# One-hot written in fp32 behind the merge, ScalarE's widening cast dropped, and the row-by-row fetch of one tile extended to every super of a graph attention kernel

## The reference

```python
h = jnp.maximum(_layernorm(x, axis=-1), 0.0)
# in _L0_gnn_ref(h, edge_index, edge_attr_64, W_node, W_edge, a):
h = (node_features @ W_node.T).reshape(num_nodes, H, HD)
e = (edge_features @ W_edge.T).reshape(num_edges, H, HD)
h_src, h_tgt = h[src], h[tgt]
att = jnp.sum(jnp.concatenate([h_src, h_tgt, e], axis=-1) * a, axis=-1)
att = jnp.where(att > 0, att, 0.2 * att)
m = jnp.maximum(jax.ops.segment_max(att, tgt, num_segments=num_nodes), 0.0)
ex = jnp.exp(att - m[tgt])
denom = jax.ops.segment_sum(ex, tgt, num_segments=num_nodes) + (num_edges - deg)[:, None] * jnp.exp(-m)
w = ex / denom[tgt]
h_prime = jax.ops.segment_sum(w[:, :, None] * h_src, tgt, num_segments=num_nodes)
return x + h_prime.reshape(num_nodes, H * HD)
```

## Time and profile before

| | before |
|---|---|
| median of 3 runs | 2087.7 us (2086.22 to 2089.43) |
| the profiled execution | 2090.56 us, its span 2088.7 us |
| GpSimd busy | 1542.5 us (74%) |
| VectorE busy | 1575.2 us (75%) |
| TensorE busy | 1460.6 us (70%), mean granted clock 0.628 |
| ScalarE busy | 768.6 us (37%) |
| bytes moved | 230.42 MB, 110 GB/s in the mean |

### The profile page before, as it was taken

How to read it: one execution, slowest core, us unless ns; L and a number is a source line. 1 busy time by engine, 2 the same in 40 slices (tenths; PEclk the granted TensorE clock), 3 DMA queues, 4 the chain that set the end, 5 groups by cost and what they waited for, 6 DMA issues and landing times.

```text
span 2088.7 us, 46636 instructions
## 1 busy us (share of the span) xinstructions
PE 1460.6 (70%) x8371; PEld 1227.2 (59%) x8372; DVE 1575.2 (75%) x4485; ACT 768.6 (37%) x2304; POOL 1542.5 (74%) x1635
## 2 busy tenths in 40 slices
PE   6456867686867776676676676677677677677685
PEld 6445656565656555565565565566566565566564
DVE  8778888787886776776776786786776786786777
ACT  7733433333343243243243243243243243243333
POOL 7777777777777777777777777777777777777770
PEclk9756767666665666566655665555655555665656
DMA  9953344343343334334334334334334333334331
GB/s 277 311 151 109 97 114 116 95 117 93 97 117 104 101 96 111 91 96 112 91 96 112 92 95 112 92 96 111 92 96 110 93 96 111 92 96 110 92 94 29
DMA packets 131275, 230.42 MB, mean 110 GB/s; under 512 B 45539, under 2 KB 90231, under 8 KB 124215
## 3 DMA queue, kind: packets, MB, share of 16 engines
q0 software_dynamic: 51968, 109.76, 23.5%
q1 hardware_dynamic: 44075, 87.75, 12.9%
q10 hardware_dynamic: 34932, 30.38, 4.5%
HBM read 182.03 MB, written 45.71 MB: 109 GB/s over the span
## 4 chain that ended last, share of the span: by engine, by line
POOL 54%; issue 22%; DVE 8%; PE 8%; ACTq 2%; ACT 2%; DMA 1%; DVEq 1%; POOLq 1%; SPq 0%
POOL gath L578 54%; PE bank_rn L1416 3%; PE bank_p L1473 2%; PE bank_w L1473 2%; DVE bank_rn L868 1%; DVE vals L988 1%; ACTq L339 1%; DVE zz L619 1%; ACT gath L1149 1%; PE bank_rn L1424 1%; DMA resets<-ef 1%; ACTq L94 1%; DVEq L94 0%; DVE vals L627 0%; SPq L455 0%
## 5 line engine op out<-in xcount | busy, mean ns | idle before, releaser
L578 POOL DMA_INDIRECT gath<-h_table,idx x1576 | 1495.2, 949 | 484.5 <-issue 478.7
L1473 PEld LDWEIGHTS bank_p<-vals,onehot 128*128 128x128 f32 x1664 | 382.9, 331 | 89.9 <-DVE vals L988 50.7
L1473 PE MATMUL bank_p<-vals,onehot 128*128 128x137 f32 x1664 | 414.0, 442 | 2.6 <-DVE vals L988 2.3
L1263 ACT ACTIVATE ab<-ab_log 128x8 f32<-128x8 f32 x209 | 43.5, 208 | 943.8 <-DVE ab_log L915 832.7
L1473 PEld LDWEIGHTS bank_w<-vals,onehot 128*128 128x128 f32 x1664 | 326.4, 287 | 94.4 <-DVE vals L988 73.0
L1473 PE MATMUL bank_w<-vals,onehot 128*128 128x137 f32 x1664 | 354.2, 393 | 23.8 <-DVE vals L988 23.3
L1449 PE MATMUL bank_s<-s_live,onehot_bits 128*128 128x24 bf16 x1672 | 79.1, 181 | 358.6 <-ACT onehot_bits L1291 358.5
L1416 PEld LDWEIGHTS bank_rn<-w_edge_bd,ef 128*128 128x128 f32 x1664 | 300.0, 282 | 15.1 <-DMA ef<-in_edges 15.1
L1416 PE MATMUL bank_rn<-w_edge_bd,ef 128*128 128x8 f32 x1664 | 294.9, 319 | 14.8 <-DMA ef<-in_edges 14.8
L1449 PEld LDWEIGHTS bank_s<-s_live,onehot_bits 128*128 128x128 bf16 x1672 | 74.2, 109 | 384.8 <-ACT onehot_bits L1291 380.4
L880 DVE SCALAR_TENSOR_TENSOR onehot_bits<-bank_w,tables,zz 128x1024 bf16 (+1 forms) x209 | 268.3, 1284 | 24.1 <-issue 5.1
(11 more groups left out here) (189 smaller groups left out, 1637.3 us busy)
## 6 DMA issues: line engine op xcount, KB each, us to landing
ef<-in_edges SPq DMA_DIRECT2D x52, 1024.0 KB
gath<-h_table SPq DMA_DIRECT2D x3256, 0.5 KB
out_x<-x_all ACTq DMA_DIRECT2D x210, 128.0 KB
gath<-h_table,idx POOLq DMA_INDIRECT x1576
gath<-h_table ACTq DMA_DIRECT2D x1480, 0.5 KB
x_all<-in_x SPq DMA_DIRECT2D x14, 448.0 KB, 12.3
out_x<-x_all SPq DMA_DIRECT2D x14, 448.0 KB
h_table<-gath SPq DMA_DIRECT2D x11, 462.0 KB
```

Of the source, the lines that this page charges most:

```text
L578: e.indirect_dma_start(gath[:, q * GPS + g, t * ROW:(t + 1) * ROW], None, table, bass.IndirectOffsetOnAxis(idx[:, q, g * TILES + t:g * TIL ...
L1473: ins = e.matmul(half_p[q], onehot[q][:, t, :], vals[q][:, t, :], start=(t == 0), stop=(t == TILES - 1))
```

## The change

- VectorE writes the one-hot straight into the fp32 buffer that TensorE reads. The bf16 copy, `widened` on ScalarE and its semaphore s_of are gone.
- The one-hot moves from before `normalise` to behind `merge`, ahead of `rescale`. `past_window` moves from behind `merge` to right behind `normalise`, ahead of vals.
- HAND_QS takes in q = 0: supers 4, 8, ..., 48 are handed too, 49 instead of 37. SyncE issues 80 rows a super (28, 28, 24), ScalarE 48 (12, 12, 12, 12).
- ScalarE's 12 rows of a step come in two portions: offsets of all 12 loaded and 4 rows issued (`rows_ahead`) before `factors`, 8 rows (`rows_behind`) at the end of the step. `store` moves from the step's end to right behind `matched`, ahead of these rows.
- Before the first one-hot VectorE waits for ScalarE's last use of that memory in the first phase.

```diff
--- before.py
+++ after.py
@@ -68,11 +68,11 @@
 LAST_TILES = -(-(N_EDGES - (GROUPS - 1) * GROUP) // P)
 LAST_LANDED = (GPS - 1) * TILES + LAST_TILES
 HAND_FIRST = 3
-HAND_QS = (1, 2, 3)
+HAND_QS = (0, 1, 2, 3)
 HANDED = [b for b in range(HAND_FIRST, SUPERS) if b % RING in HAND_QS]
 HAND_SLOT = GPS - 1
-SP_PARTS, ACT_PARTS = (32, 28, 28), (8, 8, 8, 16)
-EDGES_AT = 1
+SP_PARTS, ACT_PARTS = (28, 28, 24), (12, 12, 12, 12)
+EDGES_AT, ACT_AHEAD = 1, 4
 SP_ROWS, ACT_ROWS = sum(SP_PARTS), sum(ACT_PARTS)
 assert SP_ROWS + ACT_ROWS == P and HAND_FIRST % RING == RING - 1 and RING - 1 in HAND_QS
 ROW_BYTES = 4 * ROW
...
@@ -331,10 +330,13 @@
 
             e.sem_inc(passed, 1)
 
-        def rows_by_hand(e, landed, q, first, count):
-
-            offs = load(nc, e, hand_offs[0:1, q, first:first + count],
+        def row_offsets(e, q, first, count):
+
+            return load(nc, e, hand_offs[0:1, q, first:first + count],
                         [WINDOWS * P * ROW_BYTES - ROW_BYTES] * count)
+
+        def rows_by_hand(e, landed, q, first, offs):
+
             for k, off in enumerate(offs):
                 e.dma_start(gath[first + k:first + k + 1, q * GPS + HAND_SLOT, 0:ROW].bitcast(U8),
                             table_bytes[:, bass.ds(off, ROW_BYTES)]).then_inc(landed[q], 16)
...
@@ -510,7 +512,8 @@
                     if k == EDGES_AT and to_come:
                         next_edges(b)
                     if by_hand:
-                        rows_by_hand(e, d_hand_sp, next_q, sum(SP_PARTS[:k]), rows)
+                        first = sum(SP_PARTS[:k])
+                        rows_by_hand(e, d_hand_sp, next_q, first, row_offsets(e, next_q, first, rows))
 
             next_edges(0)
             wait(e, n_hand, 1)
...
@@ -878,7 +881,7 @@
             def one_hot(buf, slot, offset, col):
 
                 e.scalar_tensor_tensor(
-                    out=onehot_b[buf][:, :, :],
+                    out=onehot[buf][:, :, :],
                     in0=ring_p[:, bass.ds(offset, P)].rearrange("p (a j) -> p a j", a=1)
                     .to_broadcast([P, TILES, P]),
                     scalar=base[:, bass.ds(col, 1)],
...
@@ -970,9 +973,6 @@
                         in1=zs[:, ZEND:ZDST].rearrange("p (t o) -> p t o", o=1).to_broadcast(
                             [P, TILES, HEADS]), op0=ALU.max, op1=ALU.mult).then_inc(s_mc, 1)
 
-                    wait(e, s_of, s)
-                    s_col = s + 3
-                    one_hot(1 - q, *((slot_b, off_b) if q == 0 else (slot_c, off_c)), s_col)
                     if q == 0:
                         slot_c, off_c, w_past0, w_past1, slot_d, off_d = load(
                             nc, e, dve_rec[0:1, bass.ds(u, 1), :].rearrange(
...
@@ -983,6 +983,7 @@
                         beside[q][0]()
 
                     normalise(s, s_1)
+                    past_window((w_past0, w_past1)[q], s, s_1)
                     wait(e, s_ex, s_1)
                     vh = vals[q][:, :, 0:DEG].rearrange("p t (h c) -> p t h c", c=HV)
                     e.tensor_tensor(
...
@@ -997,8 +998,9 @@
                         beside[q][1]()
 
                     merge(q, s, s_1)
-                    past_window((w_past0, w_past1)[q], s, s_1)
-
+
+                    s_col = s + 3
+                    one_hot(1 - q, *((slot_b, off_b) if q == 0 else (slot_c, off_c)), s_col)
                     rescale(q, s, s_1)
                 e.reg_mov(slot_reg, slot_c)
                 e.reg_mov(slot_ahead, slot_d)
...
@@ -1073,6 +1075,7 @@
             z_columns(0, 0, False)
             wait(e, z_ready, 3)
             off_0, _, slot_1, off_1 = load(nc, e, first_rec[0:1, :], [P, SPARE, SLOTS - 1, P])
+            wait(e, n_terms, TERMS + 2)
             one_hot(0, 0, off_0, 2)
             e.reg_mov(slot_reg, 0)
             e.reg_mov(slot_ahead, slot_1)
...
@@ -1232,15 +1235,14 @@
 
                     live_s2((w_b, w_c)[q], s + 3)
                     matched(s_2)
+                    store((past_0, past_1)[q], s_1)
+                    if beside[q][1]:
+                        beside[q][1]()
+                    factors(s, s_1)
+                    if beside[q][0]:
+                        beside[q][0]()
                     if beside[q][2]:
                         beside[q][2]()
-                    factors(s, s_1)
-                    widened(1 - q, s, s_2)
-                    if beside[q][0]:
-                        beside[q][0]()
-                    if beside[q][1]:
-                        beside[q][1]()
-                    store((past_0, past_1)[q], s_1)
 
             def store(w, s_1):
 
...
@@ -1292,11 +1294,6 @@
                     "p (t c) -> p t c", c=P), ACT.Relu, bias=one[:, :], scale=-1.0
                     ).then_inc(s_e, 1)
 
-            def widened(buf, s, count):
-                wait(e, s_oh, count)
-                wait(e, s_b, s)
-                e.copy(onehot[buf][:, :, :], onehot_b[buf][:, :, :]).then_inc(s_of, 1)
-
             def feed(i, q, last_turn):
                 b, slot0 = i * RING + q, q * GPS
                 final = last_turn and q == RING - 1
...
@@ -1307,20 +1304,35 @@
 
                 next_i, next_q = (i, q + 1) if q + 1 < RING else (i + 1, 0)
 
-                def by_hand(k):
-                    if final or not handed(next_i, next_q):
+                by_hand = not final and handed(next_i, next_q)
+                offs = {}
+
+                def rows_ahead(k):
+
+                    if not by_hand:
                         return
                     if k == 0:
                         wait(e, released, b + 1)
                         settle(e)
                         e.wait_ge(d_hand_offs, (b + 1 - HAND_FIRST) * 16 + 16)
                         settle(e)
-                    rows_by_hand(e, d_hand_act, next_q, SP_ROWS + sum(ACT_PARTS[:k]), ACT_PARTS[k])
+                    first = SP_ROWS + sum(ACT_PARTS[:k])
+                    offs[k] = row_offsets(e, next_q, first, ACT_PARTS[k])
+                    rows_by_hand(e, d_hand_act, next_q, first, offs[k][:ACT_AHEAD])
+
+                def rows_behind(k):
+
+                    if not by_hand:
+                        return
+                    first = SP_ROWS + sum(ACT_PARTS[:k]) + ACT_AHEAD
+                    rows_by_hand(e, d_hand_act, next_q, first, offs[k][ACT_AHEAD:])
+
+                def parts(k, extra=None):
+
+                    return extra, lambda: rows_ahead(k), lambda: rows_behind(k)
 
                 walk(nc, e, bounds, b - 1, pair,
-                     ((None, None, lambda: by_hand(0)),
-                      (lambda: z_places(b, slot0), None, lambda: by_hand(1)),
-                      (None, None, lambda: by_hand(2)), (step_3, None, lambda: by_hand(3))))
+                     (parts(0), parts(1, lambda: z_places(b, slot0)), parts(2), parts(3, step_3)))
 
             wait(e, n_const, N_CONST + 1)
             z_places(0, 0)
```

More of the change, by code:

```diff
@@ L150, in build @@
         bits_mem = sb("onehot_bits", [P, 3, TILES, P], BF16)
-        onehot_b = [bits_mem[:, i, :, :] for i in range(2)]
         onehot_t = bits_mem[:, 2, :, :]
@@ L313, in build @@
             "DVE", "s_", "s2 xy lk dd mc oh v mn da db dg am tp ac dn rc no ou")
-        s_ex, s_de, s_e, s_of, s_ab, s_sl, s_sn, s_un, s_nd = own_sems(
-            "ACT", "s_", "ex de e of ab sl sn un nd")
+        s_ex, s_de, s_e, s_ab, s_sl, s_sn, s_un, s_nd = own_sems(
+            "ACT", "s_", "ex de e ab sl sn un nd")
         s_t, s_a, s_b = own_sems("PE", "s_", "t a b")
@@ L1330, in _ @@
             matched(1)
-            wait(e, s_oh, 1)
-            e.copy(onehot[0][:, :, :], onehot_b[0][:, :, :]).then_inc(s_of, 1)
             z_maxima(0, 0)
```

## The result

The changed kernel takes 2252.5 us, the median of 4 runs (2250.3 to 2254.1); the kernel before took 2088.6 beside it. The ratio is 1.0787, with a 95% interval of 1.0773 to 1.080: slower by 164 us. The forecast was 2263, with a range of 2140 to 2340.

What follows compares the result with a forecast made beforehand. GpSimd's gathers bound the kernel before; a ScalarE-VectorE loop would bound it after. Steps of 8.5, 9.4, 11.8 and 11.2 make 40.9 us a super; 48 supers, turns, start and end give a span of 2264, stated as 2263 (2140 to 2340).

Steps and rivals of the forecast that it cites:

- Which engine sets the pace: Whole kernel: GpSimd bounds it before; after, the consumers do, at 40.9 us a super against GpSimd's 38.75.
- One sign: Profile after: GpSimd's gathers would be held by semaphores of VectorE and TensorE instead of pure issue.
- the first rival: GpSimd stays the bound: 2073 us, needing a consumers' super of at most 36.9 us; chance 0.09 for faster.
- Part 1: GpSimd's chain loses one gather in each of 12 supers: 15 us, a gain where GpSimd stays the bound.
- Part 2: ScalarE loses the 1.03 us cast a step; VectorE's fp32 one-hot takes 1.28 us, its new place costing nothing.
- Parts 3 and 4: ScalarE's 12 rows a step and the earlier store close a loop in series with VectorE: 8.5 us inside a pair.
- a loop turn: Where the loop over supers turns, every fourth super, the boundary adds 2.4 us, 11 times.
- the super without rows: The super after super 50's z_cols, with no rows: 34 us to the next z_cols.
- The page that speaks otherwise: Skill page on issuing engines; by it 12 rows hardly lengthen a step, against 0.335 us per row DMA on ScalarE.
- Half hidden: Loop with bursts of 2.8, offsets 0.7, normalise to store 1.6: 2.6 us a super less, 2138; chance 0.10 for 2090 to 2160.
- Instructions or VectorE add: Loop lengthened by bursts of 3.3 us or a one-hot over 1.9: 2.4 us a super, 2378; chance 0.08 for over 2340.
- Part 5: SyncE's 320 rows per four supers instead of 264 cost nothing, as it waited long and issues over two supers ahead.

Runs made afterwards that it cites:

- e2: Kernel before with the one-hot in fp32 behind merge, no cast and past_window early; rows and store as before: 2099.1 us, ratio 1.0038.
- e5: Changed kernel with past_window back behind merge and the store back at the step's end, rows as changed: 2077.1 us, ratio 0.9949.
- e11: Changed kernel with past_window alone put back behind merge, the store still ahead of the 4 rows: 2596.2 us, ratio 1.2435.
- e8: Changed kernel with all 12 rows of a step ahead of ab, the store still ahead of them: 2465.0 us, ratio 1.1804.
- e10: Changed kernel with 8 rows a step by ScalarE, SyncE still at 80, 16 of 128 rows not fetched: 2078.6 us, ratio 0.996.
- e1: Changed kernel with the store alone put back at the end of ScalarE's step, behind the 8 rows: 2278.2 us, ratio 1.0906.
- e9: Changed kernel with 8 rows a step by ScalarE and 96 a super by SyncE: 2338.0 us, ratio 1.1205.
- e4: Changed kernel with all rows ahead of ab in portions of 10, 10, 10, 18 and the store last: 2185.4 us, ratio 1.0454.
- e12: As e4, changed kernel with rows ahead of ab and store last, but portions of 12, 8, 12, 16: 2078.1 us, ratio 0.9963.

## Why the prediction was right

**Which engine sets the pace** (part one, and the sum): right. z_cols waits for no gathers, ScalarE's line and VectorE make the chain. One sign came only in part: the gathers are hardly held by semaphores, 495.0 of their 594.6 us of idle time are still issue. The limit that the first rival named holds too, to 0.2 us: at paces of 35.6 to 37.6 five kernels came out at 2072 to 2079, at 39.7 the time was 2185.

**Part 1**, 12 gathers less: 1564 for the 1576 of the earlier trace rows. The 15 us were worth nothing in the change and show in the rows alone, 2087.1 - 2072.2 = 14.9.

**Part 2**, one-hot and cast: the 1.28 us were met (1277 ns), and in three of the four steps they lie in the wait for ab. In the scan step live waits for nothing; den, one step on, still waits for others there. "Nothing" for the new place is a small miss, the 8.5 us of e2.

**Parts 3 and 4**, the loop in series. Term by term, from the step shown above, beside the forecast:

| part of a step inside a pair | forecast | measured |
|---|---|---|
| ab to unseen, with 8 rows | 3.0 + 0.1 | 1001.44 - 998.66 = 2.78 |
| unseen to the end of others | 0.3 | 0.31 |
| others to den | 0.15 | 0.14 |
| den to the store | 1.9 | 1.93 |
| the store | 0.4 | 0.39 |
| the store's end to the first row | 1.0 | 1005.55 - 1004.21 = 1.34 |
| 4 rows and the step to ab | 1.65 | 1.60 |
| sum | 8.5 | 8.49 |

That this sum comes out to 0.01 is luck, because two mis-sized terms cancel: bursts of 8 took 2.6 (median of every step) and not 2.9, under the 2.8 that the forecast had as their least, and the offset loads took 0.95 to 1.25 by portion, 1.1 to 1.5 with what surrounds them, and not 1.0. Over the supers the four steps measured 8.7, 9.2, 11.25 and 11.2 for 8.5, 9.4, 11.8 and 11.2, and a loop turn added 3.7, ten times, where the forecast had 2.4, eleven times. The scan step, half a microsecond too long in the forecast, carries most of the difference. 48 supers came to 1972 instead of 1990, the super without rows to 35 instead of 34, the tail to 45.3 instead of 43: a span of 2249.5 instead of 2264. The median of the runs stands 3.0 above the span, where it was put 1 below; so the forecast was 10 high, 0.5%, with errors of both signs in it.

**The mechanism** is what the runs bear out: putting past_window and the store out of the loop gave 175 us back with the rows in place (e5); lengthening the loop by vals and merge cost 344 (e11); taking the cover of 8 rows from VectorE's work cost 213 (e8); 16 rows less a super gave 174 back (e10). What the forecast did not see is that its parts can't be undone one by one: the store alone put back ran into the landing of the store before (e1).

**The page that speaks otherwise.** A row DMA takes ScalarE 0.33 us (8 in 2.61), and four a step, with what their offsets take, were the difference between 2252 and 2079 (e10). The Trainium skill, DMA: Bandwidth & Descriptors, Issuing engines are not separate DMA queues, calls that time "usually small relative to the DMA itself". No row here sets it beside the time of the DMA itself, so this case does not refute the sentence; beside the step it is not small, 2.61 + 1.49 = 4.1 of 8.5 us.

**The other rivals.** "Half hidden": no. Its burst was met and more (2.6 for 2.8), its two other conditions were not: offsets 1.1 to 1.5 for 0.7, den to the store 1.93 for 1.6. "Instructions or VectorE add": no; the one-hot stayed in its cover. **Part 5**, SyncE at nothing: right for 80 rows a super, and not by much: at 96 it is the bound (e9).

## What to carry to other kernels

Before a wait is moved ahead of work that an engine issues in line, follow the loop that it closes through the other engine and add its terms up; here it costs 41 us a super where the same work, with the wait at the end of the step, costs 37.6. When undoing one part of a change gains nothing, look for the part that leans on it before the part is cleared. With an engine near its limit in issue time, count what a shifted row costs on both engines: 16 rows less a super on ScalarE were worth 174 us, 16 more on SyncE cost more than that.

## What was not expected of the hardware

**A register load's price goes with where it starts.** Loads of row offsets (four bytes each) that start at a multiple of 4 took 0.55 to 0.74 us for 8, 0.79 to 1.07 for 12, 1.01 for 10, 1.20 for 16, 1.49 for 14. At starts that are not, 10 took 2.39, 14 took 3.41 to 3.48 and 18 took 4.03, the same in every super within 0.3 us. These starts came only in the second and fourth step, but loads of 8 or 12 from multiples of 4 in those steps cost only 0.2 to 0.3 more than in the others. Between e4 and e12 the loads made most of 107 us. Right behind a store the 12 took 0.95 to 1.25. No run moved the start alone.

**The landing of a store varies by a factor of three.** In e1 a 128 KB store that was issued until 1023.86 let past_window go at 1028.98, 5.1 us later, where the steps before took 1.7 (1008.22 to 1009.87) and 2.6 us (1015.68 to 1018.23). The long one comes back: in 50 supers past_window waited in the scan step for the store ahead of it, and from the end of its issue to its landing the median was 4.4 us. What held it up was not tried.
